# Attention: largest values, exponentials and inverse sums signalled for each half of the heads

## What is computed

```python
q = (x @ Wq).reshape(b, n, HEADS, DIM_HEAD)
k = (context @ Wk).reshape(b, m, HEADS, DIM_HEAD)
v = (context @ Wv).reshape(b, m, HEADS, DIM_HEAD)
sim = jnp.einsum('bihd,bjhd->bhij', q, k) * SCALE
attn = jax.nn.softmax(sim, axis=-1)
out = jnp.einsum('bhij,bjhd->bihd', attn, v).reshape(b, n, HEADS * DIM_HEAD)
return out @ Wout + bout
```

## Time and profile before

| what | value |
|---|---|
| median of 3 runs | 2070.69 us (2066.13 to 2072.72) |
| the profiled execution: time | 2067.53 us |
| its span | 2065.8 us |
| TensorE busy | 1970.1 us, 95% |
| weight loads busy | 1770.5 us, 86% |
| VectorE busy | 1536.3 us, 74% |
| ScalarE busy | 1254.3 us, 61% |
| GpSimd busy | 1486.5 us, 72% |
| exponentials, L1187 | 512 activations, 180.4 us, and 512 sums read out, 122.0 us |
| reductions, L1547 | 128, 82.3 us, mean 684 ns |

### The profile page before, as it was taken

How to read it: one execution, slowest core, us unless ns; L and a number is a source line. 1 busy time by engine, 2 the same in 40 slices (tenths; PEclk the granted TensorE clock), 3 DMA queues, 4 the chain that set the end, 5 groups by cost and what they waited for, 6 DMA issues and landing times. The chain is left out here.

```text
span 2065.8 us, 50743 instructions
## 1 busy us (share of the span) xinstructions
PE 1970.1 (95%) x14320; PEld 1770.5 (86%) x14320; DVE 1536.3 (74%) x3647; ACT 1254.3 (61%) x3478; POOL 1486.5 (72%) x1695
## 2 busy tenths in 40 slices
PE   8999799999999999788999999999999999699997
PEld 6888578888887888677999999999999999678886
DVE  7888567877877787765777788888888888535554
ACT  4565466566665666534777777777777777424443
POOL 5655423776776777665888888888888888669765
PEclk9999999999999999999999999999999999889999
DMA  4300114224224323305777767677766776467543
GB/s 141 98 0 0 36 62 160 87 83 154 91 82 135 110 82 130 105 22 176 235 237 236 244 230 243 219 234 241 240 228 225 244 227 231 163 254 245 194 164 102
DMA packets 244915, 330.03 MB, mean 160 GB/s; under 512 B 50074, under 2 KB 167234, under 8 KB 244836
## 3 DMA queue, kind: packets, MB, share of 16 engines
q1 hardware_dynamic: 218788, 279.97, 41.9%
q0 software_dynamic: 26048, 49.10, 6.5%
HBM read 236.17 MB, written 77.18 MB: 152 GB/s over the span
## 5 line engine op out<-in xcount | busy, mean ns | idle before, releaser
L1362 POOL DMA_INDIRECT slot_token<-a_entry,a_slot_i x256 | 260.9, 1019 | 114.4 <-issue 70.7
L1827 POOL DMA_INDIRECT part_rows<-e_out,e_dest x184 | 222.6, 1210 | 56.8 <-issue 52.2
L2387 POOL DMA_INDIRECT x<-x_rows,tok x188 | 205.9, 1095 | 70.8 <-issue 56.6
L1958 ACT ACTIVATE e_sg<-e_g 128x256 f32<-128x256 f32 x368 | 141.3, 384 | 180.8 <-PE e_g L1675 180.1
L2007 DVE TENSOR_TENSOR e_h<-e_sg,e_u 128x256 f32<-128x256 f32 x368 | 157.1, 427 | 103.6 <-ACT e_sg L1958 48.0
L1187 ACT ACTIVATE a_prob<-a_s,a_ntop 128x128 f32<-128x128 f32 x512 | 180.4, 397 | 3.0 <-DVE a_ntop L1547 2.8
L1835 POOL TENSOR_TENSOR e_wd1l<-x,e_wd1h 128x256 fp32r<-128x256 f32 x184 | 145.9, 831 | 6.6 <-ACT e_wd1h L1938 5.7
L1835 POOL TENSOR_TENSOR e_wd0l<-x,e_wd0h 128x256 fp32r<-128x256 f32 x184 | 146.2, 831 | 2.9 <-ACT e_wd0h L1938 2.0
L1049 PE MATMUL a_o<-a_wo,a_ot 128*128 128x256 f32 x512 | 123.1, 384 | 8.4 <-DVE a_ot L1614 8.4
L2022 DVE TENSOR_SCALAR e_out<-e_d,e_dest 128x256 f32<-128x256 f32 x184 | 80.6, 479 | 59.4 <-PE e_d L1675 58.9
L1187 ACT ACTIVATION_READ_ACCUMULATOR a_prob<-a_s,a_ntop 128x1 f32 x512 | 122.0, 238 | 0.0
(11 more groups left out here) (395 smaller groups left out, 7579.7 us busy)
## 6 DMA issues: line engine op xcount, KB each, us to landing
x<-in_eg SPq DMA_DIRECT2D x94, 512.0 KB
x<-in_eu SPq DMA_DIRECT2D x94, 512.0 KB, 5.6
x<-in_ed SPq DMA_DIRECT2D x93, 512.0 KB, 5.2
part_rows<-a_zero SPq DMA_DIRECT2D x16, 2048.0 KB
x<-part_rows SPq DMA_DIRECT2D x16, 2048.0 KB, 9.5
x<-in_x SPq DMA_DIRECT2D x16, 512.0 KB, 3.8
x_rows<-x SPq DMA_DIRECT2D x16, 512.0 KB, 3.8
out_rows<-x SPq DMA_DIRECT2D x16, 512.0 KB, 9.9
```

The costliest lines, as they stand in the source:

```text
L1362: pool.indirect_dma_start(k.slot_tok, bass.IndirectOffsetOnAxis(ap=slot_i[:, j, q:q + 1], axis=0), entry[:, j, q, :], None, bounds_check=S ...
L1827: pool.indirect_dma_start(k.part_d, bass.IndirectOffsetOnAxis(ap=dest[a][:, n, 1:2], axis=0), out[a][:, n, :], None).then_inc(put[a], 16)
L1958: act.activation(sg[m % 2][:], bank_g[m % 2][:, 0:SETW], ACT.Silu).then_inc(sg_rdy, 1)
L2387: pool.indirect_dma_start(k.xg[a][:, n, :], None, k.x2_d, bass.IndirectOffsetOnAxis(ap=k.tok[a][:, n, 0:1], axis=0)).then_inc(k.rows_in[a] ...
```

## The change

The three signals between VectorE and ScalarE are given for each half of the heads. nb_rdy comes behind each reduction, and ScalarE waits for a half's largest values ahead of its four exponentials. e_rdy comes behind each four exponentials. VectorE waits for a half's exponentials, inverts its four sums, signals itself and multiplies that half, then the same for the other half. The counts of the others who wait for e_rdy and rden_rdy are doubled; scores and the shared layer's first transposes wait for the second half as they did for the whole. The number of exponentials, reductions and multiplications is the same; there are 128 inversions of 4 columns in place of 64 of 8.

```diff
@@ pe, scores @@
-                    pe.wait_ge(e_rdy, ONE + s)
+                    pe.wait_ge(e_rdy, ONE + 2 * s)
@@ pe, shared_turn @@
-                        pe.wait_ge(e_rdy, ONE + B)
+                        pe.wait_ge(e_rdy, ONE + 2 * B)
@@ act, weights @@
-                    act.wait_ge(nb_rdy, ONE + s + 1)
                     if not isinstance(s, int) or s >= 2:
                         act.wait_ge(t_done, ONE + 2 * (s - 1))
-                        act.wait_ge(rden_rdy, ONE + s - 1)
+                        act.wait_ge(rden_rdy, ONE + 2 * (s - 1))
                     for r in range(2):
+                        act.wait_ge(nb_rdy, ONE + 2 * s + r + 1)
                         for m in range(IC):
                             h = r * IC + m
                             last = act.activation(prob[b % 2][:, h, :], bank_s[r][:, m * T:(m + 1) * T], ACT.Exp,
                                                   bias=ntop[b % 2][:, h:h + 1], accum_out=den[b % 2][:, h:h + 1])
-                    last.then_inc(e_rdy, 1)
+                        last.then_inc(e_rdy, 1)
@@ dve, largest @@
-                    last.then_inc(nb_rdy, 1)
+                        last.then_inc(nb_rdy, 1)
@@ dve, shares @@
-                    dve.wait_ge(e_rdy, ONE + s + 1)
-                    dve.reciprocal(rden[:], den[b % 2][:]).then_inc(rden_rdy, 1)
-                    dve.wait_ge(rden_rdy, ONE + s + 1)
                     for r in range(2):
+                        half = slice(r * IC, (r + 1) * IC)
+                        dve.wait_ge(e_rdy, ONE + 2 * s + r + 1)
+                        dve.reciprocal(rden[:, half], den[b % 2][:, half]).then_inc(rden_rdy, 1)
+                        dve.wait_ge(rden_rdy, ONE + 2 * s + r + 1)
                         part_ = prob[b % 2][:, r * IC:(r + 1) * IC, :]
                         dve.tensor_tensor(part_, part_, rden[:, r * IC:(r + 1) * IC, None].to_broadcast([P, IC, T]),
                                           ALU.mult).then_inc(n_rdy, 1)
```

## The result

| | kernel before | with the change |
|---|---|---|
| median, us | 2070.93 (8 runs, 2066.13 to 2072.72) | 2079.70 (8 runs, 2075.57 to 2083.60) |
| ratio, 95% interval | | 1.0041 [1.0029, 1.0052] |
| profiled execution, its span | 2067.5, 2065.8 | 2083.6, 2081.9 |

The change makes the kernel 8.8 us slower, 0.4%. The forecast was no measurable change, 2072.0 with a range to 2076.7: the measured time lies above the range.

The account below looks back on a forecast made before the run. TensorE's own work was taken to bound the attention stage, except its start and end. Terms -0.6 + 1.65 + 0.22 = +1.3 us on the 2070.7 median gave 2072.0 us, range 2064.7 to 2076.7.

Parts of the forecast that it names:

- the inversion for each half: VectorE, every attention slot: a second inversion with its signal and wait adds 0.22 us, bounds 0.19 and 0.26.
- The costly step: Rival: the added VectorE step costs about 0.5 us a slot, not 0.22, giving 2078.2 us; chance 0.07.
- the -0.4 with the shorter step: Alternative sum if a 4-element inversion takes the skill's estimated 0.065 us, so the step stays within the slack at group boundaries.
- the term of +1.65 us: Eleven group boundaries: the 0.22 step exceeds a 0.07 slack, so TensorE's q load comes 0.15 us late each; bounds 0 and 2.9.
- The -0.6 us at the start: Attention stage's start: exponentials begin about 0.6 us earlier, after the first half's reduction; bounds -0.6 and -0.3.
- The last slot's +0.22 us: Stage's end: the last slot's doubled inversion lies in VectorE's unbroken chain to the last attention output copy, adding 0.22 us.
- ScalarE's cover: Other 63 slots: ScalarE's copies of transposed weights hide the earlier largest values, gain 0; without cover, at most 0.6 a slot.
- The ways named to see it wrong: Groups between 416 and 808 us unchanged, or over 0.4 us longer, or TensorE's idle time changed in slots not at boundaries.
- The clock rival: Stage's start or end: shifted waits remove or add a 2.7 us TensorE half-clock stretch, giving 2069.3 or 2074.7; chance 0.25.

Follow-up runs that it names:

- the run with two increments: Two semaphore increments added on VectorE ahead of its loop over groups, in the kernel before: 2077.55 us, ratio 1.0032.
- the padding spread: The change plus 48 semaphore increments on VectorE, four in each of the twelve slots before its loop: 2069.81 us, ratio 0.9998 to the kernel before.
- the run with 64 increments: The change plus 64 semaphore increments in one place on VectorE, at the attention stage's start ahead of its loop: 2077.47 us, ratio 1.003 to the kernel before.
- the two padded versions of the kernel before: The kernel before with 2 or 8 semaphore increments on VectorE ahead of its loop: 2077.55 and 2082.10 us.
- the three kernels that refetch: The change, 2079.70 us, and the kernel before with 8 or 2 semaphore increments ahead of VectorE's loop, 2082.10 and 2077.55 us.

## Why the prediction was wrong, point by point

**The failed step is the inversion for each half.** The prediction called it "the only work that is added", and priced the 64 inversions by their duration and by the slack behind them. It added up what VectorE executes and left out what VectorE has to load: in two groups' body 24 more instructions, for which it set no term and no bound. None of the rivals held it either. The costly step, the one rival on the slower side (2078.2), came near the measured time by a mechanism that isn't there: the step is not 0.5 us but 0.21, from 415.97 to 416.17 and then 454.94 to 455.15 in the rows above. What the runs showed in its place: the loop's code is fetched anew at each of five jumps back, five packets each, VectorE stands for 1.7 to 2.2 us, and TensorE waits for it; with the clock's fall that made 11.7 us in the profile and about 8.8 in the median. The signs that the prediction could have read were the 41 packets of code on the page before, a loop of 303 instructions in the trace, and an edit that lengthens it. That this loop lay at an edge could not be read there; the run with two increments found it.

**The size of the step was right.** 0.22 was forecast; 0.20 to 0.21 stands in the rows, and 128 inversions of four columns take 144 to 178 ns each, the 0.18 taken from the earlier trace rows. The forecast distance of 0.82 between the two multiplications is 455.15 - 454.33 = 0.82. The prediction's other sum, the -0.4 with the shorter step, keeps 0.22 for the last slot; with the shorter step there too it is -0.5.

**The slack behind it was mis-sized, and the term of +1.65 us is not there in the run that isolates it.** The step took the least distance from the subtraction's end to the load as 0.12, from the earlier trace rows. With the padding spread it is 455.83 - (454.50 + 1.27) = 0.06: the slack was 0.13 and not 0.07. The load comes 0.04 later than in the kernel before, and the turn is no longer. In the run with 64 increments some turns did grow, to 78.2 us from 77.9, but not by the 0.15 a group of the forecast: the 0.3 stands whole in one group of two, and in that group a conversion in the choice of experts is three times its usual length. The same line in this run, then with the padding spread:

```profile
533.21 0.47 DVE L1471 CAST a_esel<-a_eidx 128x16 f32<-128x16 uint32 x1
```

```profile
448.21 0.17 DVE L1469 CAST a_esel<-a_eidx 128x16 f32<-128x16 uint32 x1
```

The four groups with the long conversion grew by 0.3, the fifth with a jump, where it took 0.18, by nothing. From 416.92 to the load ten groups later at 808.51 the kernel with the padding spread takes 391.59 us, the kernel before 391.66: the term is 0 there. What the second inversion did take is the slack: another delay of 0.3 on VectorE then reached TensorE whole. Why the conversion was long there is not known.

**The -0.6 us at the start came.** ScalarE's idle time ahead of its first exponential fell from the 2.75 of the earlier trace rows to 2.16, and TensorE's wait behind it from 4.3 to 3.7:

```profile
257.81 0.37 ACT L1187 ACTIVATE a_prob<-a_s,a_ntop 128x128 f32<-128x128 f32 x1 [2.16 <-DVE a_ntop L1547]
```

**The last slot's +0.22 us is not resolved.** TensorE's wait for the last copy is 8.4 us after, 8.37 before, and 7.5 to 8.4 among the other kernels; a term of 0.2 drowns in that.

**ScalarE's cover held but for the branch.** The prediction said that ScalarE's own order holds the exponentials in the steady slots. Its waits for the largest values are 6.1 us in six after, against 2.8 in one; the five new ones, some 0.8 each, stand behind the five gaps of VectorE, and with the padding spread one of 2.2 is left. So the earlier signals gain nothing in the steady state, as forecast.

**The ways named to see it wrong did fire.** "I am wrong if the groups between 416 and 808 us (...) grow by over 0.4 us": they grew by 11.7 / 10 = 1.2 on average, and unevenly: measured from load to load, by 1.8 to 3.4 us in the group that holds the branch and by less than 0.1 in the one behind it. The 3.4 is the group with the lower clock. (The group ahead of these ten is 0.6 longer, 0.5 of it a wait for GpSimd's counting.) A per-slot cost would have been even; the unevenness with the loop's own period is what pointed to the code.

**The clock rival came in a place it had not named.** It looked at the stage's start and end and put a stretch at 2.7 us. In the kernel after the clock fell once inside the steady groups, near 667 us, for about 1.5 us of the loss. TensorE had stood idle for 1.95 us just before, for GpSimd's counting; the kernel before has the same idle time there without a fall, so what tips it was not found.

**What stays open.** The profiled execution lost 11.7 us over these ten groups, the medians differ by 8.8, and the two padded versions of the kernel before, with the same five packets for each jump, lost 6.6 and 11.2. VectorE's wait at a jump is 1.7 to 2.2 us in the kernel after, and with eight increments ahead of the kernel before it is 1.8 at most. The clock's falls are one part of what differs; what sets the rest was not tried.

## What to carry to other kernels

Count an edit inside a hardware loop twice: by the time of its instructions and by their number. Read the packets of the engine's instruction queue on the page before and after, and look for an idle time marked "issue" at the loop's head; here it came once for each jump back. When an edit of no weight costs some us, repeat the kernel before with a few empty instructions ahead of its loop, and the edit with its code moved or the loop written out, before blaming the work. Put such padding where the engine has idle time: 64 increments in front of a step that others wait for cost 5 us of their own and hid the answer.

## What the runs showed of the hardware that was not expected

- Two semaphore increments ahead of a loop of 303 instructions turned a loop that loads nothing into one that loads five packets of 8 KB for each jump back, and cost 6.6 us over five jumps.
- An engine that is busy 74% of the time and bounds nothing (VectorE) makes the bounding one wait for up to 1.9 us a turn, since at the boundary of two groups TensorE has only 0.13 us of slack against it.
- A semaphore increment on VectorE is recorded at 21 ns and not counted as busy, but 64 in a row stood 0.1 us apart, 6.2 us together, and appear only as idle time marked "issue" ahead of the next instruction. 48 of them in slots with idle time cost nothing that the time shows.
- In the three kernels that refetch, TensorE's granted clock fell in the middle of a stage that is otherwise at full clock (0.96 on average over a group of 40 to 45 us), for about 1.5 us each time.
- Writing the loop out puts 49 packets on the queue in place of 41, and costs nothing that the time shows (0.9994 of the kernel before).
